# Time mixing of a two-layer sequence model: exponent pairs from one difference, products moved from GpSimd to VectorE, input loaded by batch item

## What is computed

```python
rvk = einsum('btc,dc->btd', layernorm(x), W_rvk); r, v, k = split(rvk, 3)
def step((aa, bb, pp), (kt, vt)):
    ww = u + kt;  p = maximum(pp, ww)
    e1 = exp(pp - p);  e2 = exp(ww - p)
    y = (e1 * aa + e2 * vt) / (e1 * bb + e2)
    ww2 = pp + w;  p2 = maximum(ww2, kt)
    e1 = exp(ww2 - p2);  e2 = exp(kt - p2)
    return (e1 * aa + e2 * vt, e1 * bb + e2, p2), y
out = einsum('btc,dc->btd', sigmoid(r) * wkv, W_out)
```

## Time and profile before

| | us |
|---|---|
| median of 3 runs | 1811.97 (1806.33 to 1815.72) |
| the profiled execution | 1816.28 |
| its span in the trace | 1814.5 |
| last `x_state` of time mixing ends at | 128.87 |
| first transformer matmul starts at | 133.32 |

### The profile page before, as it was taken

The page is one execution under the profiler, slowest core; times in us unless marked ns, Lnnn a source line. Parts: engine busy times, 40 slices in busy tenths (PEclk is TensorE's granted clock), DMA queues, the critical chain, the costliest instruction groups (busy, mean ns, idle before and its releaser), DMA issues. The chain is left out here.

```text
span 1814.5 us, 75400 instructions
## 1 busy us (share of the span) xinstructions
PE 1625.9 (90%) x31933; PEld 1249.7 (69%) x32029; DVE 1490.1 (82%) x3214; ACT 1097.0 (60%) x1971; POOL 1013.0 (56%) x932
## 2 busy tenths in 40 slices
PE   2547999989999989999989999989999989999975
PEld 1225777777777767777767777768777767777753
DVE  6859988888888788888888888888888888888841
ACT  2215666666766656666656666766667656767641
POOL 4416655585455485565585565585556575556510
PEclk8659999999999999999999999999999999999996
DMA  3011111111111121011111011111101111101101
GB/s 96 23 35 34 35 36 38 58 47 39 39 31 38 47 58 38 23 47 38 46 58 38 23 47 39 58 46 39 47 24 39 58 46 38 46 24 39 35 14 47
DMA packets 39012, 74.94 MB, mean 41 GB/s; under 512 B 8944, under 2 KB 19992, under 8 KB 38680
## 3 DMA queue, kind: packets, MB, share of 16 engines
q1 hardware_dynamic: 38680, 70.11, 13.1%
HBM read 20.08 MB, written 2.10 MB: 12 GB/s over the span
## 5 line engine op out<-in xcount | busy, mean ns | idle before, releaser
L662 POOL TENSOR_TENSOR qk<-qk,qk_sin 128x512 f32<-128x512 f32 x384 | 490.9, 1278 | 208.1 <-DVE qk_sin L736 208.1
L670 POOL TENSOR_TENSOR qk<-qk,rnorm 128x512 f32<-128x512 f32 x384 | 400.4, 1043 | 368.9 <-DVE rnorm L773 368.9
L913 ACT ACTIVATE squares<-bank 128x512 f32<-128x512 f32 x384 | 229.0, 596 | 167.7 <-DVE qk_sin L736 165.6
L1039 PE MATMUL bank<-w_hi,xs_hi 128*128 128x512 f32 x576 | 290.2, 504 | 13.1 <-ACT squares L913 7.7
L746 DVE TENSOR_REDUCE norm<-squares 128x8 f32<-128x512 f32 x384 | 258.5, 678 | 30.6 <-ACT squares L913 28.5
L730 DVE TENSOR_TENSOR qk<-bank,tables 128x512 f32<-128x512 f32 x384 | 261.8, 682 | 5.8 <-PE bank L1041 5.8
L736 DVE TENSOR_TENSOR qk_sin<-bank,tables 128x512 f32<-128x512 f32 x384 | 261.5, 681 | 0.0
L1049 PE MATMUL bank<-ident,qk 128*128 128x128 f32 x1536 | 236.5, 277 | 8.8 <-POOL qk L670 6.9
L1041 PE MATMUL bank<-w_hi,xs_lo 128*128 128x512 f32 x576 | 229.6, 399 | 1.2 <-issue 1.2
L1040 PE MATMUL bank<-w_lo,xs_hi 128*128 128x512 f32 x576 | 227.9, 396 | 0.8 <-issue 0.8
L1049 PEld LDWEIGHTS bank<-ident,qk 128*128 128x128 f32 x1536 | 184.6, 141 | 56.2 <-POOL qk L670 8.0
(11 more groups left out here) (139 smaller groups left out, 2629.5 us busy)
## 6 DMA issues: line engine op xcount, KB each, us to landing
v<-v SPq DMA_DIRECT2D x96, 390.0 KB, 3.5
v<-v SPq DMA_DIRECT2D x72, 130.0 KB, 3.4
w_raw<-in_L_ffn_Wqkv SPq DMA_DIRECT2D x36, 256.0 KB, 3.4
w_o_s<-in_L_ffn_Wo SPq DMA_DIRECT2D x6, 512.0 KB, 5.4
w_s<-in_L_ffn_W SPq DMA_DIRECT2D x6, 341.0 KB, 4.8
x_res_scratch<-mix_x_res SPq DMA_DIRECT2D x4, 256.0 KB, 2.4
f_x_res<-x_res_scratch SPq DMA_DIRECT2D x4, 256.0 KB, 3.6
out<-f_o_nat SPq DMA_DIRECT2D x4, 256.0 KB, 2.4
```

Source lines behind the costliest of these rows:

```text
L662: pool.tensor_tensor(qk[:, g % 2, c, :], qk[:, g % 2, c, :], qk_sin[:, c, :], ALU.add).then_inc(added[c], 1)
L670: pool.tensor_tensor(view, view, rnorm[:, g % 2, c * HPC:(c + 1) * HPC].unsqueeze(2) .to_broadcast([P, HPC, DH]), ALU.mult).then_inc(norme ...
L913: act.activation(squares[:, c % 2, :], bank_of(Q0 + c)[:], ACT.Square).then_inc(squared[c], 1)
L1039: pe.matmul(bank_of(c)[:], l_hi, w_hi[:, cols], start=True, stop=False)
```

## The change

The recurrence is rewritten with one difference for each pair of exponentials. With xd = (pp + w) - k, the new e2 is exp(-max(xd, 0)) and the new e1 is exp(-max(-xd, 0)); the same with yd = (k + u) - pp for f1 and f2. ACT does the rectifiers, so it has eight activations for each item and not four. `d1`, `d2`, `pk`, `g1` and `g2` are gone. All products are on DVE; POOL is left with the weight splits, which now wait for `den2_ready`, and gets three Newton steps of the second root (12 small instructions for an item) after DVE has made the seed. The last item's second root is eight small steps on DVE, as is the first layer norm's. x comes in four DMAs, and item 0 has its statistics taken alone. PE widens the root with transposes; the copy of `vecs`, `ident_bf` and `mask_bf` goes to ACT. The order on each engine is new:

```diff
+            load_x(0)
+            sp.dma_start(ident[:], ident_in).then_inc(loaded_w, 16)
...
+            for b in range(1, BATCH):
+                load_x(b)
...
-                pool.tensor_tensor(d2[:, p], k_s[:, p], pp[:, p, 1:], ALU.subtract).then_inc(d2_ready, 1)
...
-                pool.tensor_tensor(g1[:, p], pp[:, p, 0:SEQ], pk[:, p], ALU.subtract).then_inc(g1_ready, 1)
...
-                pool.tensor_tensor(f2v[:, p], f2[:, p], v_s[:, p], ALU.mult).then_inc(f2v_ready, 1)
...
-                pool.tensor_tensor(f1b[:, p], f1[:, p], bb[:, p, 0:SEQ], ALU.mult).then_inc(f1b_ready, 1)
+            def newton(b):
...
+                pool.wait_ge(seeded, b + 1)
+                for n in range(3):
+                    seq(pool.tensor_tensor(s, v_, y, ALU.mult))
+                    seq(pool.tensor_tensor(s, s, y, ALU.mult))
+                    seq(pool.tensor_scalar(s, s, -0.5, 1.5, ALU.mult, ALU.add))
+                    if n < 2:
+                        seq(pool.tensor_tensor(y, s, y, ALU.mult))
+                pool.tensor_tensor(y, s, y, ALU.mult).then_inc(rs_ready, 1)
...
+            for b in range(BATCH):
+                weights.arrived(pool, 0, 2 + b)
+                pool.wait_ge(den2_ready, b + 1)
+                weights.split(pool, 0, 2 + b)
+                newton(b - 1)
...
+                dve.scalar_tensor_tensor(xd[:, p], pp[:, p, 0:SEQ], w_neg[:], k_s[:, p], ALU.add,
+                                         ALU.subtract).then_inc(xd_ready, 1)
...
+                dve.scalar_tensor_tensor(yd[:, p], k_s[:, p], first[:], pp[:, p, 0:SEQ], ALU.add,
+                                         ALU.subtract).then_inc(yd_ready, 1)
...
+            def weigh_output(b):
...
+                dve.tensor_tensor(f2v[:], f2[:, p], v_s[:, p], ALU.mult).then_inc(f2v_ready, 1)
...
+                dve.tensor_tensor(f1b[:], f1[:, p], bb[:, p, 0:SEQ], ALU.mult).then_inc(f1b_ready, 1)
...
+            statistics(0, NBLK)
+            layer_norm(0)
+            for b in range(1, BATCH):
+                dve.wait_ge(loaded_x[b], 16)
+            statistics(NBLK, BATCH * NBLK)
+            layer_norm(1)
...
+            scan_maximum(0)
+            for b in range(BATCH):
+                layer_norm(b + 2)
+                scale_state(b - 2)
+                scan_state(b)
+                scan_maximum(b + 1)
+                residual(b - 1)
+                weigh_output(b)
+                seed(b - 1)
+                divide(b)
+            b, p = BATCH - 1, (BATCH - 1) % 2
+            scale_state(b - 1)
+            residual(b)
...
+                act.activation(e2[:, p], xd[:, p], ACT.Relu).then_inc(act_seq, 1)
+                act.activation(e1[:, p], xd[:, p], ACT.Relu, scale=-1.0).then_inc(act_seq, 1)
...
+            for b in range(BATCH):
+                take_x(b + 2)
+                take_k(b + 2)
+                exponentials(b + 1)
+                take_centred(b - 1)
+                take_vr(b + 2)
...
+            for b in range(BATCH):
+                turn_x(b + 2)
+                project(b + 2)
+                centre(b - 1)
+                output(b)
+                widen(b - 1)
```

More of the change, by code:

```diff
@@ L87, in need @@
         eng.wait_ge(sem, value)
[L90 to L109, removed]
 class Chain:
@@ L258, in rounds @@
-        def rounds():
-            for t in range(BATCH + 2):
-                yield tuple(b if 0 <= b < BATCH else None for b in (t, t - 1, t - 2))
+        xd, yd, e1, e2, f1, f2, rwkv, x_res, xc, xsq = (sb(name, [P, 2, SEQ]) for name in (
+            "xd", "yd", "e1", "e2", "f1", "f2", "rwkv", "x_res", "xc", "xsq"))
+        e2v, f1a, f2v, f1b, num, den, rden = (sb(name, [P, SEQ]) for name in (
+            "e2v", "f1a", "f2v", "f1b", "num", "den", "rden"))
+        loaded_x = [sem(f"loaded_x{b}") for b in range(BATCH)]
@@ new lines, in divide, with residual @@
+            def divide(b):
+                dve.wait_ge(den2_ready, b + 1)
+                dve.reciprocal(rden[:], den[:]).then_inc(rden_ready, 1)
+                dve.wait_ge(rden_ready, b + 1)
+                dve.wait_ge(num_ready, b + 1)
+                need(dve, o_ready, b - 1)
+                dve.tensor_tensor(rwkv[:, b % 2], num[:], rden[:], ALU.mult).then_inc(rwkv_ready, 1)
+            def residual(b):
+                if not real(b):
+                    return
+                p = b % 2
+                dve.wait_ge(o_ready, b + 1)
+                dve.wait_ge(xt_evac, 2 * b + 2)
+                need(dve, stored[p], 16 * (b // 2))
+                need(dve, cen_ready, b - 1)
+                dve.tensor_tensor(x_res[:, p], bank[5][:], x_t[:, b], ALU.add).then_inc(res_ready, 1)
@@ new lines, in output, with widen @@
+            def output(b):
+                pe.wait_ge(rwkv_ready, b + 1)
+                need(pe, res_ready, b)
+                pe.matmul(bank[5][:], w_out_t[:], rwkv[:, b % 2], start=True, stop=True).then_inc(o_ready, 1)
+            def widen(b):
+                if not real(b):
+                    return
+                pe.wait_ge(rs_ready, b + 1)
+                pe.wait_ge(cen_evac, 2 * b + 2)
+                for j in range(NBLK):
+                    mm = pe.transpose(bank[6][:, j * P:(j + 1) * P],
+                                      rstd2[:, b % 2, j:j + 1].to_broadcast([P, P]), ident[:])
+                mm.then_inc(bc_ready, 1)
```

465 lines of the change are left out of this document (248 added, 217 removed).

## The result

The change runs in 1794.85 us (median of 4 runs, 1788.45 to 1803.52) against 1813.85 for before beside it (4 runs): ratio 0.9891, 95% interval 0.986 to 0.9922, so 1.1% faster. A second set of 6 runs gave 0.9914 (0.9885 to 0.9943). Forecast were 1785.0 us and 1776 to 1798. The direction is right and the time lies in the range, but a third of the forecast gain of 27 us is missing in the median, and the profiled executions say where: 1793.4 us of span instead of 1814.5, 21.1 less.

A forecast was written before the change was run, and what follows sets the result against it. DVE's stream was taken to bound time mixing; gains of 9.1 + 18.4 + 0.8 = 28.3 us, less 1.3 for collisions, left 27.0: 1789.3 profiled, median 1785.0 us, range 1776 to 1798 (forecast's own 1780 to 1790).

The forecast's parts named there:

- What bounds: Time mixing: DVE's stream sets an item's cost, so each microsecond taken from it comes off the end.
- Start: Up to item 0's `rwkv`: first maximum scan at 16.6 us, not 25.02; `rwkv` ends at 35.3, not 44.4; gain 9.1.
- Items: Items 1 to 3 of time mixing: 16.9, 19.5 and 16.2 us with new waits; gains 7.7, 4.3 and 6.3, together 18.4.
- Rival B: PE at its upper clock level: projection and transposes take half, 8 us more gain, 1777; chance 0.12.
- Newton steps: Second root on POOL: 12 instructions at 0.3 us, 3.6 in all, late only above 0.46 us each.
- A: POOL's small instructions take 0.738 us, Newton chains hold `x_state` back, some 11 us less gain: 1796; chance 0.14.
- C: POOL's Newton instructions take 1.26 us each, chain 15.6 us per item, 31.7 lost in all: 1817; chance 0.03.
- Tail: After item 3's `rwkv`: 12.7 us to the end of the last `x_state` against 13.5, gain 0.8.
- collisions: DVE and POOL still blocking each other, from early weight splits, tables and 36 small POOL instructions: 1.3 us off the gain.
- Rectifiers at nothing: Rectifiers on ACT cost nothing beyond a first wait in item 0; 16 on DVE would add 9.8 us to its stream.
- the same distance from there to the end of the run: Transformer: the time from the last `x_state` to the end stays as before.
- rival D: The stage ends 27 us sooner and the transformer gives it back, say by a late weight piece: 1812; chance 0.03.

The follow-up runs named there:

- the experiment with one load: The change with all of x loaded in one transfer again; last `rwkv` ends at 92.33 us against 89.75, one run.
- before again: The kernel before, unedited, run a second time; ratio to before 0.9996 (0.9975-1.0017).
- change again: The changed kernel, unedited, run a second time; ratio to before 0.9914 (0.9885-0.9943).
- and early residual: Root widened first, plus the residual ahead of the next maximum scan on DVE and ACT's square ahead of its exponentials; ratio to before 0.9884.
- change + 26 empty: The change with 26 do-nothing TensorE instructions (52 waits on a raised semaphore) added behind `project(1)`; ratio to before 0.9846.
- before + 230 empty: The kernel before with 230 do-nothing TensorE instructions (460 waits) added behind the turning of the weights; ratio to before 1.0132.
- Root widened first: The change with PE widening each root ahead of the next output projection and DVE's state scans ahead of `x_state`; ratio to before 0.9864.
- its padded form: Root widened first with 26 do-nothing TensorE instructions added after the second item's projection; 1779.7 us, ratio to before 0.9799.

## Why the prediction was right, and where it failed

**What bounds.** Right. DVE's stream sets the item: what was taken from it came off the end of the stage, and what the experiments put on it (rectifiers) or what slowed it (POOL's products) came back.

**Start.** Predicted 16.6 for the first scan and 35.3 for the first `rwkv` end, measured 17.20 and 36.54. The terms given for the first scan add up to 16.2 and not 16.6; what the measured 17.20 has beyond them is one collision, `mix_var` at 1.14 us beside POOL where the same form takes 0.17. A second one, the scan of `bb` at 1.75 instead of 1.20, follows it. The gain is 7.9 instead of 9.1, and the experiment with one load gives the load by batch 2.5 of it.

**Items.** `xd` is 0.75 (0.74 predicted), the wait ahead of `x_state` 3.02 (3.1), ahead of the variance 1.45, 1.87 and 1.11 (1.8, 1.8, 1.1). Items 1 to 3 take 16.79, 19.54 and 16.88 us, forecast 16.9, 19.5 and 16.2; they gain 7.9, 4.2 and 5.6, in sum 17.7 of 18.4. The 0.7 of the last is one collision again: its seed step takes 0.85 us beside POOL's weight split instead of 0.16. Rival B (upper clock) fell in the items: the stretch that holds one has 0.50:

```profile
53.00:72.00 19.00, 6.87 (x16) 3.66 (x16) 14.04 (x18) 5.22 (x10) 4.05 (x13) 0.50 0.09 28
```

(length of the stretch, then busy us of PE, PEld, DVE, ACT and POOL, granted clock, DMA share and GB/s).

**Newton steps.** Taken at 0.3 us for want of a row; the timeline of POOL has them at 0.20, and 0.28 from start to start, so that 12 end after 3.28 us, well ahead of the projection. Rivals A and C (0.738 and 1.26 us each) fall with it:

```profile
49.43 0.20 POOL L294 TENSOR_TENSOR mix_nt<-mix_var,mix_rstd 128x4 f32<-128x4 f32 x1
...
52.51 0.20 POOL L299 TENSOR_TENSOR mix_rstd<-mix_nt,mix_rstd 128x4 f32<-128x4 f32 x1
```

**Tail.** 11.08 us after the last `rwkv` instead of 12.7, and that is luck of the clock, rival B in this one place. In the first profile DVE waits 3.13 us for the last variance, at a granted clock of 0.65 in the tail; in the change's repeat it waits 4.72 at 0.50, and the tail is 12.67, the forecast. So at the clock from which the prediction read its rows the stage gives 26.5 us (128.87 to 102.37), not 28.0: 9.1, 18.4 and 0.8 were forecast, less 1.3 for collisions; 7.9, 17.7 and 0.8 came, with the collisions in them. They cost 2.6 us at the four places shown, twice their term.

**Rectifiers at nothing.** Right in place, they lie beside the products. On DVE they cost 2.5 us and not the 9.8 that I worked out from the two-input pitch of 0.61: with one input the pitch is 0.34, and waits gave some back.

**The step that failed** is "the same distance from there to the end of the run", with "the kernel's steady part does not change" said against rival D. The program of the transformer does not change, but its place among TensorE's instructions did: 26 fewer ahead of it. The pauses moved by 13 pairs within the score bursts, and the stretch up to the last row maximum took 13 us more, some 10 of them by the places of the pauses. A higher granted clock gave 6.7 back behind it. Rival D thus happened by a quarter, through a mechanism that I had not listed (no weight piece was late). That places of the pauses set the time is shown from both sides, by 26 instructions added to the change and 230 to before. The median stayed in the range of 1776 to 1798 only by the width that it had for other reasons: 1794.85 is outside the 1780 to 1790 of the forecast itself.

**What TensorE waits for in the pauses** can be read from the traces. The page's list of DMA queues has one named "instruction", with 257 packets and 4.21 MB:

```profile
q8 instruction: 257, 4.21, 1.0%
```

Each packet is 16,384 bytes, and the trace of the change's repeat has 65,869 TensorE instructions, some 256 for each packet (before with 230 empty ones has 66,125 and 258 packets). In the eleven traces that have all records of matmuls (the first ones of before and change lack 96), every idle moment of the weight loads within a burst stands ahead of the 194th or 195th TensorE instruction of such a group of 256, and none anywhere else in 12,288 pairs. In all 13 traces each pause over 0.9 us, 356 of them, ends 1.2 to 1.8 us after a packet of that queue has landed, where packets come some 6 us apart. So these are waits for the supply of instructions, at every 256th. In sum they are:

| run | idle at these places | row maxima | of it at 1.2 GHz | from the last row maximum to the end | clock there |
|---|---|---|---|---|---|
| before again | 45.0 | 1595.9 | 27.3 | 57.6 | 0.71 |
| change again | 60.1 | 1605.0 | 20.5 | 53.3 | 0.84 |
| and early residual | 58.8 | 1606.0 | 27.3 | 56.4 | 0.75 |
| change + 26 empty | 41.4 | 1587.9 | 13.7 | 60.3 | 0.68 |
| before + 230 empty | 60.9 | 1612.6 | 37.5 | 56.2 | 0.75 |

Of the 15.1 us between the repeats of before and of the change, 8.1 are at 15 places that had no idle time within a burst in before: eleven of them stood at pair 51 to 61 of a burst and stand, 13 pairs further, at pair 0 to 10 of the next. The other 7.0 are at the 40 places that both have.

**Open.** Why the supply comes late at one of these places and not at another, and why the same pause is longer on average 13 pairs further into a burst (1.30 against 1.12 us), is not shown. Row maxima start when a burst's matmuls are done, so a pause near the end may have less work behind which to hide; that is only argued. Nor is it known why the granted clock behind the last row maximum lies between 0.68 and 0.87 from run to run; that it sets this part's length is what the two rows of the result show.

## What to carry to other kernels

Rebuild the stream of the bounding engine from durations it has when no other engine disturbs it; here this came within 1.3 us at each item's end but the last, and 1.9 there. Compare two executions at a point that TensorE's clock has not moved, here at the last `rwkv` and not at the last `x_state`. Before work is moved off the bounding engine, ask whether it stood in a wait, and what the other engine's instructions hold up; and ask what covers each chain moved off it: here POOL's Newton steps were free only under the reciprocal. And where TensorE runs through long bursts without waits, compare the unedited stage too: the number of instructions ahead of it is part of its time, and a version should be judged at a few such offsets before one says that an edit brought little.

## What the runs showed of the hardware

- TensorE pauses in bursts at every 256th of its instructions, for 0 to 3.6 us, waiting for instructions: the places are the same in each execution of a program, and a 16 KB packet of the instruction queue has landed 1.2 to 1.8 us before each pause over 0.9 us ends. 26 instructions more moved this kernel's time by 0.5 to 0.7% (0.9891 and 0.9914 to 0.9846, and 0.9864 to 0.9799; the intervals overlap in part, the traces agree), and adding 230 to before, 256 more than the change has, gave the change's places.
- Products of 128x512 on POOL and two-input forms or scans on DVE hold each other up: `xd` 1.57 instead of 0.75 us, the maximum scan 2.22 instead of 1.20. A form with one tensor input was held up too, `mix_var` with 1.14 instead of 0.17. Even 4-column steps on POOL took up to 1.04 us instead of 0.20 under DVE's scans and products. The Trainium skill (SBUF — State Buffer, SBUF: two separate sides) has this as a lock for a whole instruction, when VectorE has two SBUF inputs or runs in a mode with two ports; the rows with two inputs agree in kind.
- TensorE's granted clock differed in the tail of time mixing between executions of like programs. Root widened first had 0.94 there, its padded form 0.50, that is nearly all at 2.4 GHz against 1.2; the same steps to the last variance took 2.96 and 4.72 us. The window of the first:

```profile
85.30:89.20 3.90, 2.46 (x12) 1.38 (x11) 0.87 (x3) 1.28 (x3) 0.00 (x0) 0.94 0.20 71
```

and of the second:

```profile
87.00:91.10 4.10, 3.19 (x10) 1.78 (x8) 0.16 (x1) 1.07 (x2) 0.00 (x0) 0.50 0.17 64
```
